# The operand of a weight matmul built along the free axis by ScalarE and transposed whole, in place of rows copied inside SBUF

## What is computed

```python
w_m = (efeat @ W_msg + b_msg).reshape(E, 16, 16)
w_a = (efeat @ W_attn + b_attn).reshape(E, 16, 16)
h_src = x[src][:, :, None]
e1, e2 = w_m * h_src, w_a * h_src
ex = exp(e2 - segment_max(e2, dst)[dst])
ft = segment_sum(e1 * ex / segment_sum(ex, dst)[dst], dst).sum(axis=1)
x = layernorm(x + ft)
x = layernorm(x + segment_sum(efeat, dst) / counts)
```

## Time and profile before

| | |
|---|---|
| median of 3 runs | 3736.78 us (3733.45 to 3740.55) |
| the profiled execution | 3747.97 us, span 3746.0 us |
| TensorE busy | 2266.3 us (60%), mean granted clock 0.805 |
| VectorE busy | 1868.6 us (50%) |
| ScalarE busy | 1294.7 us (35%) |
| GpSimd busy | 1681.8 us (45%) |

### The profile page before, as it was taken

How to read it: one execution, slowest core, us unless ns; L and a number is a source line. 1 busy time by engine, 2 the same in 40 slices (tenths; PEclk the granted TensorE clock), 3 DMA queues, 4 the chain that set the end, 5 groups by cost and what they waited for, 6 DMA issues and landing times.

```text
span 3746.0 us, 22137 instructions
## 1 busy us (share of the span) xinstructions
PE 2266.3 (60%) x6671; PEld 932.4 (25%) x6671; DVE 1868.6 (50%) x3011; ACT 1294.7 (35%) x1186; POOL 1681.8 (45%) x1759
## 2 busy tenths in 40 slices
PE   5211566656655566666576665575766575766786
PEld 0100122222222222222222222232322232222232
DVE  6711454445544444554455455464545464555574
ACT  2000233333333333333243343243434343443354
POOL 4276444444444443345435535445354544544520
PEclk9955688878887777887788788787888787878898
DMA  8110000000000000000000000000000000000000
GB/s 259 49 17 13 13 14 14 13 14 14 17 14 13 13 13 13 13 17 14 12 13 18 12 14 17 13 13 16 14 16 14 15 17 12 16 13 14 16 12 15
DMA packets 83834, 79.36 MB, mean 21 GB/s; under 512 B 36001, under 2 KB 65814, under 8 KB 83147
## 3 DMA queue, kind: packets, MB, share of 16 engines
q0 software_dynamic: 63584, 41.26, 6.2%
q1 hardware_dynamic: 20124, 36.60, 3.3%
HBM read 55.66 MB, written 2.01 MB: 15 GB/s over the span
## 4 chain that ended last, share of the span: by engine, by line
another core or an unknown queue 31%; PE 24%; DVE 21%; issue 16%; ACT 5%; POOL 1%; DMA 1%; DVEq 0%; SPq 0%; POOLq 0%; ACTq 0%
PE PX L909 17%; DVE AR L1191 11%; PE PW L895 6%; DVE AR L1204 4%; PE PTB L883 1%; ACT AR L745 1%; ACT PX L743 1%; POOL AR L582 1%; ACT L716 1%; DVE AR L1064 1%; ACT LT L706 1%; DVE AR L1208 1%; DVE AR L1162 1%; DVE AR L1177 1%
## 5 line engine op out<-in xcount | busy, mean ns | idle before, releaser
L582 POOL DMA_INDIRECT AR<-in_xt,AR x1600 | 1530.3, 956 | 1771.7 <-DVE AR L1191 1211.4
L1191 DVE CUSTOM_DVE_ANT_1 AR<-PW,AR 128x1024 f32<-128x1024 f32 x812 | 974.4, 1221 | 1645.4 <-remote 1242.5
L909 PE MATMUL PX<-AR,CS 128*128 128x512 f32 x3248 | 1712.6, 655 | 72.7 <-issue 69.7
L895 PE MATMUL PW<-WS,LT 100*128 100x512 bf16 x1624 | 554.4, 428 | 1258.1 <-DVE AR L1191 744.6
L909 PEld LDWEIGHTS PX<-AR,CS 128*128 128x128 f32 x3248 | 679.2, 210 | 712.4 <-issue 604.8
L706 ACT ACTIVATE LT<-PTB 48x1024 bf16<-48x1024 bf16 (+1 forms) x220 | 209.1, 951 | 1637.6 <-remote 1058.0
L1204 DVE TENSOR_TENSOR AR<-AR,PX 128x1024 f32<-128x1024 f32 (+1 forms) x440 | 499.8, 1136 | 134.0 <-ACT PX L743 109.4
L895 PEld LDWEIGHTS PW<-WS,LT 100*128 100x128 bf16 x1624 | 127.3, 101 | 1729.2 <-issue 880.5
L745 ACT ACTIVATE AR<-AR 128x2048 f32<-128x2048 f32 (+1 forms) x220 | 428.6, 1948 | 7.2
L749 ACT ACTIVATE PX<-AR 128x1024 f32<-128x1024 f32 (+1 forms) x220 | 214.4, 975 | 572.4 <-issue 285.1
L743 ACT ACTIVATE PX<-AR 128x1024 f32<-128x1024 f32 (+1 forms) x220 | 231.1, 1050 | 14.0 <-DVE AR L1204 12.5
(11 more groups left out here) (113 smaller groups left out, 560.6 us busy)
## 6 DMA issues: line engine op xcount, KB each, us to landing
AR<-in_xt,AR POOLq DMA_INDIRECT x1600
LT<-LT SPq DMA_DIRECT2D x152, 64.0 KB
AR<-in_ea SPq DMA_DIRECT2D x3, 3128.0 KB, 15.1
LT<-LT SPq DMA_DIRECT2D x152, 32.0 KB
LT<-LT SPq DMA_DIRECT2D x68, 48.0 KB
AR<-in_ea SPq DMA_DIRECT2D x1, 3120.0 KB, 12.6
LT<-fl_d SPq DMA_DIRECT2D x152, 2.0 KB
LT<-LT SPq DMA_DIRECT2D x68, 24.0 KB
```

What stands on the lines that cost most here:

```text
L582: g.indirect_dma_start(feat(h, j - j0, j - j0 + 1), None, xt, bass.IndirectOffsetOnAxis(ap=XE[:, lo + 17 * j:lo + 17 * j + 1], axis=0))\
L895: i = pe.matmul(PAIRS[s % 2][:, j, :], LT[:, g % 3, lo:lo + 128], WS[:, :], start=True, stop=True)
L909: i = pe.matmul(PDR, IDN, x, start=(a == 0 and j == 0), stop=(g == LAST[k] and j == n - 1))
L1191: v.tensor_tensor_reduce(em(g, j, j + 2).rearrange("p (x c) -> p x c", c=32), w, hb, 1.0, LOW, ALU.mult, ALU.max, accum_out=MXC[:, k % 2, ...
```

## The change

ScalarE writes the 100 columns of every slot into a new tile `XP` along the free axis, twice or three times where a part is repeated, and TensorE transposes all 100 at once. `evac` copies 100 rows instead of 48. SyncE's three DMAs per group go, and so do the table of flags (L873, L1141, L1142), its store (L409) and its wait. The edges are cleared in place in `XE`, so `XE` is now read by `diff`, `mean` and ScalarE, and `runs_of` waits for these. The core of the diff:

```diff
@@ buffers @@
-        RCT = reg([128, DEG[0] + DEG[1], 48])
+        RM = reg([128, DEG[0], 16])
+        XP = reg([128, DEG[0] + DEG[1], K], bf16)
@@ SyncE @@
-                sp.wait_ge(S["v_flg"], 1)
-                sp.dma_start(FLD2, FLT2.rearrange("p j q -> p (j q)")).then_inc(S["d_flg"], 16)
+                sp.wait_ge(S["d_y"], 16 * NC)
                 sp.dma_start(XNN, xt[0:NP, :].rearrange("(p c) k -> p c k", c=NC)).then_inc(S["d_xn"], 16)
-                sp.wait_ge(S["d_flg"], 16)
-
-                def copies(g):
...
-                for g in range(NGR):
-                    copies(g)
-                sp.wait_ge(S["d_y"], 16 * NC)
@@ GpSimd @@
                 def runs_of(k):
                     if k >= 2:
-                        g.wait_ge(S["v_ev"], k - 1)
+                        g.wait_ge(S["v_x1"], k - 1)
+                        g.wait_ge(S["v_sa"], k - 1)
+                        g.wait_ge(S["a_p"], 4 * (k - 2) + 3)
...
                 runs_of(0)
+                g.memset(XP[:, :, 96:99], 1.0).then_inc(S["g_m"], 1)
+                g.memset(XP[:, 0:roff[1] + 1:roff[1], 99], 0.0).then_inc(S["g_m"], 1)
@@ ScalarE @@
-                    a.activation(LT[0:48, g % 3, 0:128 * n], PTB[0:48, 0:128 * n], ACT.Copy).then_inc(S["a_T"], 1)
+                    a.activation(LT[:, g % 3, 0:128 * n], PTB[0:K, 0:128 * n], ACT.Copy).then_inc(S["a_T"], 1)
...
+                def first(k):
+                    d = DEG[k]
+                    a.wait_ge(S["v_ev"], k + 1)
...
+                    a.activation(part(k, 99, 100)[:, 1:d, :], VLD[:, 1:d].unsqueeze(2), ACT.Relu, bias=1.0, scale=-1.0).then_inc(S["a_p"], 1)
+                    h = upper(edge(k))
+                    a.activation(part(k, 0, 96).rearrange("p j (x w) -> p j x w", x=2)[:, :, :, 0:16], twice(h), ACT.Copy)\
+                     .then_inc(S["a_p"], 1)
+                    a.activation(part(k, 80, 96), h, ACT.Copy).then_inc(S["a_p"], 1)
+
+                def second(k):
+                    a.wait_ge(S["v_x1"], k + 1)
...
+                    a.activation(part(k, 0, 96).rearrange("p j (x w) -> p j x w", x=2)[:, :, :, 16:32], twice(upper(RM[:, 0:DEG[k], :])),
+                                 ACT.Copy).then_inc(S["a_p"], 1)
...
+                        if p == FIRST[k] - 4:
+                            first(k)
+                        if p == FIRST[k] - 3:
+                            second(k)
@@ TensorE @@
+                    pe.wait_ge(S["a_p"], 4 * k + 4)
...
-                        i = pe.transpose(PTB[0:48, 128 * j:128 * j + 128], rct(k)[:, j0 + j, :].bitcast(bf16)[:, 1::2], IDB[:, :])
+                        i = pe.transpose(PTB[0:K, 128 * j:128 * j + 128], part(k, 0, K)[:, j0 + j, :], IDB[:, :])
...
-                        pe.wait_ge(d_lt[g % 3], 48 * (g // 3 + 1))
@@ VectorE @@
-                v.tensor_tensor(FLT2, DEGT.unsqueeze(1).broadcast_to([NC, BINS, 128]),
-                                IOTA[0:NC, 0:BINS].unsqueeze(2).broadcast_to([NC, BINS, 128]), ALU.is_le).then_inc(S["v_flg"], 1)
...
+                    v.tensor_tensor(edge(k), edge(k), VLD[:, 0:d].unsqueeze(2).broadcast_to([128, d, 16]), ALU.mult)\
+                     .then_inc(S["v_ev"], 1)
...
+                    v.tensor_tensor(part(k, 32, 48), x, upper(x), ALU.subtract).then_inc(S["v_x3"], 1)
```

More of the change, by code:

```diff
@@ L119, in gnn_kernel @@
     YD = nc.dram_tensor("y_d", [NP, 32], f32, kind="Internal").ap()
-    FLD2 = nc.dram_tensor("fl2_d", [NC, BINS * 128], bf16, kind="Internal").ap()
     DTD = nc.dram_tensor("dt_d", [ZROW + 1, DW], f32, kind="Internal").ap()
@@ L295, in gnn_kernel @@
         OUTR = reg([128, NC, 32])
-        XNN = reg([128, NC, 16])
         RCG = reg([128, NC])
@@ L306, in gnn_kernel @@
         STN = EMR[:, 16 * NC * 5:16 * NC * 5 + 4 * NC].rearrange("p (x c) -> p x c", c=NC)
+        XNN = EMR[:, 16 * NC * 6:16 * NC * 7].rearrange("p (c w) -> p c w", w=16)
         SUF = sb("SUF", [128, BINS])
@@ L310, in gnn_kernel @@
         VIO = sb("VIO", [128, 1])
-        FLT2 = FLTW.bitcast(bf16).rearrange("p (j q) -> p j q", q=128)
         PW = ctx.enter_context(nc.psum_tensor("PW", [128, 4, 512], f32))
@@ L373, in feat, with edge, part, upper @@
             return HGF[:, hoff[k % 3] + 16 * (j0 + lo):hoff[k % 3] + 16 * (j0 + hi)]
-        def rct(k):
-            return RCT[:, roff[k % 2]:roff[k % 2] + DEG[k], :]
+        def edge(k):
+            lo = 17 * roff[k % 2]
+            return XE[:, lo:lo + 17 * DEG[k]].bitcast(f32).rearrange("p (j w) -> p j w", w=17)[:, :, 1:17]
+        def part(k, lo, hi):
+            return XP[:, roff[k % 2]:roff[k % 2] + DEG[k], lo:hi]
+        def upper(x):
+            return x.bitcast(bf16)[:, :, 1::2]
+        def twice(x):
+            return x.unsqueeze(2).broadcast_to([128, x.shape[1], 2, 16])
         block = ctx.enter_context(nc.Block())
@@ L729, in half @@
                     return EXP[:, 0:16 * w].rearrange("p (x o) -> p x o", o=16)
+                def first(k):
+                    d = DEG[k]
+                    a.wait_ge(S["v_ev"], k + 1)
+                    if k >= 2:
+                        a.wait_ge(S["p_T"], LAST[k - 2] + 1)
+                    a.activation(part(k, 99, 100)[:, 1:d, :], VLD[:, 1:d].unsqueeze(2), ACT.Relu, bias=1.0, scale=-1.0).then_inc(S["a_p"], 1)
[5 more added lines that the diff above has]
+                    a.wait_ge(S["v_x1"], k + 1)
+                    if k >= 2:
+                        a.wait_ge(S["p_T"], LAST[k - 2] + 1)
+                    a.activation(part(k, 0, 96).rearrange("p j (x w) -> p j x w", x=2)[:, :, :, 16:32], twice(upper(RM[:, 0:DEG[k], :])),
+                                 ACT.Copy).then_inc(S["a_p"], 1)
                 a.wait_ge(S["g_m"], 6)
+                first(0)
+                second(0)
                 evac(0)
@@ L735, in regular @@
                     p, c = STEPS[i] if i < len(STEPS) else (None, None)
+                    for k in range(1, NC):
+                        if p == FIRST[k] - 4:
+                            first(k)
+                        if p == FIRST[k] - 3:
+                            second(k)
                     if i - 2 in FINS:
@@ L871, in regular @@
                 i.then_inc(S["p_perm"], 1)
-                pe.wait_ge(S["v_tab"], 1)
-                pe.transpose(PMB[0:NC, 0:128], DEGR[:, :], IDN).then_inc(S["p_deg"], 1)
+                pe.wait_ge(S["g_m"], 9)
                 pe.wait_ge(S["d_w2"], 160)
@@ L1160, in diff @@
                     v.wait_ge(S["v_ev"], k + 1)
-                    x = rct(k)[:, :, 0:16]
-                    v.tensor_tensor(rct(k)[:, :, 16:32], x, x.bitcast(bf16)[:, :, 1::2], ALU.subtract).then_inc(S["v_x1"], 1)
+                    if k >= 1:
+                        v.wait_ge(S["a_p"], 4 * k)
+                    v.tensor_tensor(RM[:, 0:DEG[k], :], edge(k), upper(edge(k)), ALU.subtract).then_inc(S["v_x1"], 1)
                 def low(k):
                     v.wait_ge(S["v_x1"], k + 1)
-                    x = rct(k)[:, :, 16:32]
-                    v.tensor_tensor(rct(k)[:, :, 32:48], x, x.bitcast(bf16)[:, :, 1::2], ALU.subtract).then_inc(S["v_x3"], 1)
+                    if k >= 2:
+                        v.wait_ge(S["p_T"], LAST[k - 2] + 1)
+                    x = RM[:, 0:DEG[k], :]
+                    v.tensor_tensor(part(k, 32, 48), x, upper(x), ALU.subtract).then_inc(S["v_x3"], 1)
                 def floors(lo, hi):
@@ L1207, in mean @@
                     v.wait_ge(S["v_ev"], k + 1)
[L1208 removed]
+                    v.tensor_reduce(OUTR[:, k, 16:32], edge(k).rearrange("p j i -> p i j"), AX.X, ALU.add).then_inc(S["v_sa"], 1)
                 def weigh(k):
```

25 lines of the change are left out of this document (5 added, 20 removed).

## The result

The changed kernel took 3702.04 us (median of four runs, 3699.14 to 3706.26), the kernel before 3735.14 us beside it. The ratio is 0.991, 95% interval 0.9893 to 0.9927: 33 us less, where 80 us were forecast. That is small, 0.9%, but clear of the noise. The profiled execution took 3706.26 us, with a span of 3704.4 us against 3746.0.

The account below looks back on a forecast made before the run. TensorE's results were taken to come late while GpSimd issues long gather bursts. From the profiled 3748 us, −2 (copies), −123 (pauses) and +45 (ScalarE) gave −80, so 3668, less 11 for the median: 3657 us, range 3520 to 3810.

Parts of the forecast that it names:

- the term for the pauses, −123: GpSimd's moved wait breaks gather bursts in two; 16 tiles gain a clean start, −123 us, bounds 0 and −323.
- The two regimes: TensorE starts 3.5 matmuls per us when clean, 0.82 from about 10 us into a gather burst to 5 us after.
- a pause starts a clean stretch afresh: After a GpSimd pause TensorE again runs about 10 us at full rate; a pause of 3.65 us was enough.
- the place of a burst is nothing: Rival: pauses gain nothing and ScalarE's work decides; slower, 3807 us, or 3780 with its +45 us; chance 0.27.
- −7.7 us for a tile with a clean start: Per tile whose first gathers follow a fresh pause, the slow stretch is 10 us shorter, worth −7.7 us.
- Together 16 × −7.7: Tiles 4 to 6 and 23 to 35 counted as ending after the burst's second part; −123 us in all.
- just separate: 30-slot tiles, 30 to 35: end at 31 us against the second part's 30, so 6 × −7.7 us.
- Joined: 0: Tiles ending before the burst's second part is over: it runs into the next first part, burst as long as before, 0 us.
- First and last tiles: 0: The moved GpSimd wait changes nothing in the first and last tiles, 0 us.
- ScalarE's writes, +45: ScalarE's column writes, 3 us a tile, 145 us in all, mostly hidden by VectorE's slack; +45 us, bounds 0 and +145.
- The transpose's weight load, 0: TensorE's load growing from 48 to 100 columns, 1624 times, costs 0 us; upper bound +166 us.
- Copies and flags, −2 at the start: Removing SyncE's copies and flags gains 0 us in the tiles and 2 us at the start.

Follow-up runs that it names:

- wait-alone kernel: Kernel before, plus one wait: GpSimd fetches a tile's edges only after VectorE's mean of two tiles earlier; 3702.79 us against 3754.39 (chip A).
- the kernel with the pause in one piece: Changed kernel, plus a GpSimd wait for the mean ahead of each tile's first gather; 3767.53 us, ratio 1.0028 to the kernel before.

## Why the prediction was right or wrong

The direction was right, and so was the cause: the place of GpSimd's pause gives the gain. The size was wrong by 47 us, because the term for the pauses, −123, was far too large. Step by step:

- **The two regimes, and that a pause starts a clean stretch afresh.** Right for the chip of the first measurement and for A, if the pause is long enough for the burst before it: the same gathers in shorter bursts are worth 12%. Rival "the place of a burst is nothing" falls there. The rule of the Trainium skill cited with it (SBUF — State Buffer, Who interferes with whom: TensorE never waits for another engine) is about ports of SBUF. Taken as the prediction's rival took it, that GpSimd's bursts have no effect, it fails on chip A, and the trace of C agrees with it: there TensorE starts 35 matmuls in 10 us of gathers and 93 in the next 33. That ports have to do with what is seen on A isn't shown.
- **−7.7 us for a tile with a clean start.** Right: 7.3 us a tile over tiles 27 to 34 of the wait-alone kernel; 13.9 and 9.9 in the two such tiles of the changed kernel. That it came out so close is in part luck: these starts had 13 to 30 matmuls in their first 10 us, not the 39 of the earlier trace rows.
- **"Together 16 × −7.7".** This is the step that failed. I counted a tile as separate when its end came after the second part, by any margin. The pause that I went by, 3.65 us in the earlier trace rows, stood behind a burst of eight gathers, inside a clean stretch; I used it for pauses behind a second part of some 30 us, in a slow one. There 1.7 to 3.0 us of idle GpSimd gave 5 matmuls in the next 10 us (1.1 to 2.3 us with the wait alone gave 1 to 11), and 3.9 us or more gave 13 to 30. The 32-slot tiles, which I put 7.5 us behind the second part, came 0.3 to 4.8 us behind it in the changed kernel, the 30-slot ones, "just separate", up to 6.0. Only tiles 26 and 32 had a clean start, for −24 us together. In the wait-alone kernel it was nine tiles (27 to 34 and 47), for −66 us.
- **"Joined: 0".** Also wrong. Where the parts join, a tile's first eight gathers fall into the slow stretch's end (no matmul at all in 2105.6 to 2115.6), and the pause comes too late to be used in full. Tiles 4 to 24 lost 17.2 us in the changed kernel, 32.3 with the wait alone. The whole term, −123, measured −52 by the wait alone.
- **"First and last tiles: 0".** Wrong too, and here it helped the forecast: tiles 1 to 3 gained 18.1 us in the changed kernel and 15.1 with the wait alone, and tiles 36 to 47 of the changed kernel 12.1, with no clean start among them. Why those last ones gained stays open.
- **ScalarE's writes, +45.** Its time on the engine was right (3.19 us a tile). Its price on the path was not measured cleanly on a chip like A: 12 us by the times, 35 by the ratios, all of it in the four tiles that lose their cleaner start. On C it is nothing. VectorE waits for L763 113.5 us in the changed kernel, where the kernel before had 109.4 for the same copy, so it is not there that it is paid.
- **The transpose's weight load, 0.** The load grew by 25 ns; times 1624 that is 41 us on the queue of loads. The rule cited from the Trainium skill (TensorE: Matmul & The Clock Gate, Weight-path perf modes) speaks of a load that gets longer, and the trace agrees in direction: 100 columns take 133 ns against 101 for the 128 of `LT`. (The bf16 loads of 128 columns by 128 partitions near the start, 64 of them, take 126 ns, so 101 ns isn't the time of every load of 128 columns.) The 25 ns are under the 43 estimated from it. No run took it away, so its price is open; on C, where one wait accounts for the cost of the change, nothing of it shows.
- **Copies and flags, −2 at the start.** Tile 0 was 4.0 us shorter, and as short in the kernel with the pause in one piece, but not with the wait alone; so this gain is the rest of the change. TensorE's wait for the landings gave nothing, as costed.

The sum by what was measured: −52 for the wait (on A), −33 for all (first measurement), so by these differences the rest cost about 19 us and not the 43 that I had. The times themselves, 3702.79 and 3702.04 us, are equal; the two were never measured side by side on a chip like A.

## What to carry to other kernels

Where one engine's bursts slow another down, a pause has value only where it is long enough for the burst before it, and a moved wait can join two bursts as easily as split one: compute the idle time ahead of each burst, not its order, and ask for a margin. Where idle time is cheap, spread the work on purpose, by holding each piece to the consumer's count a fixed number of groups back, rather than leave it to the buffers. And measure on more than one chip before a mechanism is believed: the wait that gains 1.4% on one costs 0.9% on another, and pacing that gains 12% on one costs, with a distance one shorter, 0.6% on another.
